# Refilling the gather indices of an edge loop by SyncE transfers inside SBUF instead of GpSimd copies

## The reference

```python
proj = (x @ Wp.T).reshape(-1, H, FO)                      # 6250 x 8 x 32
s = leaky_relu(scores_src[src] + scores_trg[trg], 0.2)    # one score an edge and head
exp_s = exp(s - max(s))
denom = segment_sum(exp_s, trg, N)
out = segment_sum(proj[src] * (exp_s / (denom[trg] + 1e-16))[:, :, None], trg, N)
```

## Time and profile before

| what | value |
|---|---|
| time, median of 3 runs | 3241.75 us (3241.1 to 3244.08) |
| profiled execution: span from the first to the last instruction | 3796.4 us |
| of it the edge loop, first gather to the end of the last | 247.76 to about 2809 us |
| busy in the whole span: PE, DVE, ACT, POOL | 56%, 52%, 23%, 48% |

### The profile page before, as it was taken

The page is one execution under the profiler, slowest core; times in us unless marked ns, Lnnn a source line. Parts: engine busy times, 40 slices in busy tenths (PEclk is TensorE's granted clock), DMA queues, the critical chain, the costliest instruction groups (busy, mean ns, idle before and its releaser), DMA issues. The chain is left out here.

```text
span 3796.4 us, 46157 instructions
## 1 busy us (share of the span) xinstructions
PE 2122.9 (56%) x12432; PEld 1788.7 (47%) x12433; DVE 1956.5 (52%) x5386; ACT 890.4 (23%) x2271; POOL 1821.9 (48%) x2025
## 2 busy tenths in 40 slices
PE   3755454544545554545455455444543359999990
PEld 3434343433434443434334334333433359999990
DVE  6545444444444444444444444444458746666654
ACT  1221111111111111111111111111114435555540
POOL 1026655656556656656565565655635722222110
PEclk7976767677777667677677776776765579999995
DMA  1333322323233333323333333322324442222116
GB/s 54 113 96 84 86 80 81 85 78 85 80 81 83 86 83 85 84 81 83 81 84 81 81 83 83 85 80 80 85 63 144 117 118 65 68 90 67 44 44 207
DMA packets 163652, 326.51 MB, mean 86 GB/s; under 512 B 41487, under 2 KB 95742, under 8 KB 163628
## 3 DMA queue, kind: packets, MB, share of 16 engines
q0 software_dynamic: 98560, 256.53, 24.7%
q1 hardware_dynamic: 45528, 50.33, 4.4%
q10 hardware_dynamic: 19540, 19.40, 1.6%
HBM read 278.03 MB, written 47.99 MB: 86 GB/s over the span
## 5 line engine op out<-in xcount | busy, mean ns | idle before, releaser
L626 POOL DMA_INDIRECT rows<-proj_table,idx x1568 | 1492.1, 952 | 1028.6 <-DVE weighed L741 612.9
L670 PE MATMUL banks<-weighed,onehot 128*128 128x264 f32 x3136 | 1147.8, 528 | 1293.5 <-DVE weighed L741 1232.4
L670 PEld LDWEIGHTS banks<-weighed,onehot 128*128 128x128 f32 x3136 | 783.1, 263 | 1475.0 <-issue 1312.5
L725 DVE TENSOR_REDUCE target<-banks 128x32 f32<-128x96 f32 x393 | 100.6, 256 | 1193.0 <-remote 1108.5
L741 DVE TENSOR_TENSOR weighed<-rows,banks 128x1024 f32<-128x1024 f32 x392 | 474.5, 1211 | 0.0
L845 ACT ACTIVATE banks<-score,neg_bound 128x32 f32<-128x32 f32 x392 | 114.1, 291 | 1387.8 <-DVE score L734 1069.5
L840 ACT CAST onehot_t<-banks 128x512 bf16<-128x512 f32 x395 | 228.2, 578 | 764.3 <-remote 740.0
L1441 POOL DMA_INDIRECT results_by_token<-yrow,goes_to x104 | 109.1, 1049 | 478.2 <-DVE yrow L1389 350.7
L707 DVE TENSOR_TENSOR onehot<-banks,key_tab 128x512 f32<-128x512 f32 x397 | 270.9, 683 | 0.0
L1328 ACT ACTIVATE hid<-banks,params 128x256 f32<-128x256 f32 x416 | 197.9, 477 | 267.5 <-PE banks L1284 261.1
L1284 PE MATMUL banks<-f_xth,w1h 128*128 128x256 f32 x832 | 236.4, 284 | 27.2 <-ACT hid L1328 14.9
(11 more groups left out here) (236 smaller groups left out, 2901.1 us busy)
## 6 DMA issues: line engine op xcount, KB each, us to landing
rows<-proj_table,idx POOLq DMA_INDIRECT x1568
w_raw<-in_L_ffn_W_dram POOLq DMA_DIRECT2D x16, 1024.0 KB
xrow<-tokens_by_expert SPq DMA_DIRECT2D x106, 128.5 KB
c_y<-results_by_token SPq DMA_DIRECT2D x10, 1120.0 KB
proj_table<-trow ACTq DMA_DIRECT2D x50, 128.9 KB
xin<-in_x_dram SPq DMA_DIRECT2D x50, 125.0 KB
skip_rows<-srow ACTq DMA_DIRECT2D x50, 125.0 KB
r_skin<-skip_rows SPq DMA_DIRECT2D x10, 625.0 KB
```

The costliest lines, as they stand in the source:

```text
L626: nc.gpsimd.indirect_dma_start(rows[k][:, i, :], None, table, bass.IndirectOffsetOnAxis(ap=idx[pair][:, col:col + 1], axis=0)).then_inc(ga ...
L670: mm = nc.tensor.matmul(acc_bank[u // 2 % 2][:, 0:ROW], onehot[u][:, i, :], weighed[:, k * SET + i, :], start=(u % 2 == 0 and i == 0), sto ...
```

## The change

The four copies of a round leave GpSimd. SyncE gets a loop of its own over the rounds. For each pair it waits until the gathers of both its sets have landed (the semaphores `gathered`, which DVE waits for too), and then refills that `idx` tile for the next round by a transfer from `src_tab`, inside SBUF: 128 partitions of 32 bytes. The first four tiles are filled by four such transfers ahead of the loop. GpSimd waits, at the first set of each pair as before, for `idx_ready[pair]`, which now counts 16 a transfer. The table's tail is made long enough for the refill behind the last round (32 columns instead of 24). Behind a pass GpSimd also waits for those last refills, and SyncE waits for `forgotten` before it goes on.

```diff
             act.wait_ge(src_out, EC)
-            nc.scalar.copy(m["src_tab"][:, STEPS * G:(STEPS + AHEAD) * G], m["src_tab"][:, 0:AHEAD * G])
+            nc.scalar.copy(m["src_tab"][:, STEPS * G:STEPS * G + ROUND * SET], m["src_tab"][:, 0:ROUND * SET])
...
             def body(c, it, w):
                 at = counts(pool, c, 2)
-                one_more = value_of(pool, c + 1)
-
-                def sources(pair):
-                    nc.gpsimd.tensor_copy(idx[pair][:], m["src_tab"][:, bass.ds(ROUND * SET * it + pair * 2 * SET, 2 * SET)]
-                                          ).then_inc(idx_ready[pair], 1)
-
-                sources(0)
+                copied = value_of(pool, 16 * c + 16)
                 for u in range(ROUND):
                     k, pair = u % BUF, u // 2
                     pool.wait_ge(begun, 1)
                     if u % 2 == 0:
-                        pool.wait_ge(idx_ready[pair], one_more)
+                        pool.wait_ge(idx_ready[pair], copied)
                     pool.wait_ge(weigh_done[k], at(u))
...
-                    if u % 2 == 0 and u + 2 < ROUND:
-                        sources(pair + 1)
 
             def forget_gathers(w):
                 used = value_of(pool, 2 * IT * (w + 1) + 1)
+                copied = value_of(pool, 16 * IT * (w + 1) + 16)
                 pool.wait_ge(begun, 1)
+                for pair in range(ROUND // 2):
+                    pool.wait_ge(idx_ready[pair], copied)
...
         @block.sync
         def _(sp):
+            def sources(pair, first):
+                sp.dma_start(idx[pair][:], m["src_tab"][:, bass.ds(first + pair * 2 * SET, 2 * SET)]
+                             ).then_inc(idx_ready[pair], 16)
+
+            def body(c, it, w):
+                landed = [value_of(sp, 16 * SET * (2 * it + q + 1)) for q in range(2)]
+                following = sp.snap(ROUND * SET * it + ROUND * SET)
+                for pair in range(ROUND // 2):
+                    for u in (2 * pair, 2 * pair + 1):
+                        sp.wait_ge(gathered[u % BUF], landed[u // BUF])
+                    sources(pair, following)
+
+            def forget_landings(w):
+                passed = value_of(sp, w + 1)
+                sp.wait_ge(forgotten, passed)
+                sp.sem_inc(resumed, 1)
+
+            for pair in range(ROUND // 2):
+                sources(pair, 0)
             for done in m["spent_by_nodes"]:
                 sp.sem_clear(done)
+            over_passes(sp, body, forget_landings)
```

More of the change, by code:

```diff
@@ L52 @@
 COLS = EC * P * Q
-assert (STEPS + AHEAD) * G <= COLS
+assert (STEPS + AHEAD) * G <= COLS and STEPS * G + ROUND * SET <= COLS
 NO_NODE = 16384
@@ L583, in edge_phase @@
             "st_picked", "st_ready", "acc_added", "max_masked", "max_kept"))
-        peak_dve, peak_pe, windows_moved, forgotten = (sem(s) for s in (
-            "peak_dve", "peak_pe", "windows_moved", "forgotten"))
+        peak_dve, peak_pe, windows_moved, forgotten, resumed = (sem(s) for s in (
+            "peak_dve", "peak_pe", "windows_moved", "forgotten", "resumed"))
         begun = m["begun"]
```

## The result

The changed kernel takes 3191.64 us (median of 4 runs, 3190.28 to 3194.89) against 3241.45 before: 0.9842 of the time, 95% interval 0.983 to 0.9853. It is 49.8 us faster. The forecast was 3206 us and 36 us; its lowest end, 3191 us of 3241.75, is a ratio of 0.9843, just above what was measured.

What follows compares the result with a forecast made beforehand. POOL was taken to pace the edge loop in the timed runs. Mid-round copies -13, copies at the turn -32, SyncE's issues +7 and the start +2 gave -36 us, so 3206 us (1.1% less); range 3191 to 3242.

Steps and rivals of the forecast that it cites:

- the copies at the turn: Edge loop, top of each round: 48 copies on POOL at 0.67 us each, 32 us gone; other end 10 us.
- POOL paces the timed loop: Edge loop: a POOL that never waits takes 2011 us; the profile's 550 us more are pauses absent from timed runs.
- Rival A: Edge loop: waits for DVE and PE also fill timed runs, a quarter of the saving or less left, 3232 to 3242; chance 0.12.
- Copies by their place: POOL's gathers in the edge loop: a copy costs 0.67 us at the turn of a round, 0.09 in mid-round.
- The mid-round copies: Edge loop, three copies a round on POOL, 147 in all at 0.09 us each: 13 us gone.
- SyncE's issues: Edge loop, 196 refills issued beside POOL's gathers: 0.035 us each, +7 us (0 to +69).
- The start: Ahead of the loop: the first gather now waits for a transfer, +1 to +3 us, taken as +2.
- The profiled span: Profile after the change: falls by far less than 36 us; wait for weighed rows grows over 612.9 us.
- Slack of the refill: SyncE's refills in the loop: due 30 us later, landing 2.4 to 3.9 us after issue, some 24 us free.

## Why the prediction was right, and where it was wrong

The mechanism held, and the size did not: 36 us were forecast and 49.8 measured, a ratio of 0.9842 just past the 0.9843 of the range's lowest end. The step that failed is the term for the copies at the turn. It was put at 32 us, with 10 as its other end, and measured 36 to 38.

**POOL paces the timed loop: right, shown.** The forecast rested on taking the profiled execution's 550 us of pauses for something that the timed runs don't have. The profile taken again has a loop of 2013 us, within 2 us of the sum over POOL's distances. Rival A falls. That the sums met so closely was in part luck. The plain distance is 1.250 us in that profile and not 1.254, 6 us less over the loop, and the turns cost 6 us more than the sum gave them. Outside the loop the two executions differ too: 1226 us, where the prediction took the 1235 of the first profile for both.

**Copies by their place: right, shown.** 0.67 us at the turn, 0.09 to 0.10 in mid-round, as read. The wait for a copy just made is dear, not the turn.

**What is off is sizes.** 49.8 - 36 = 14 us were missed, in three terms that together make 15. The mid-round copies are 14 us by the rows where 13 stood. A few us go the other way: the changed kernel's distances are 1.2527 us on the mean, and the plain ones of the second profile of before 1.250. That isn't SyncE's doing, as the two variants with as many of its issues or four times as many have 1.2508 and 1.2505, and the two profiles of before differ by as much (1.253 and 1.250).

- *SyncE's issues, +7 us: measured 0.* The 0.03 us came from three distances of another phase, with other work around them. In the changed kernel, distances with an issue of SyncE are no longer than those without, and 588 more issues changed nothing.
- *The start, +2 us: measured about 0.* From the ACT table load that opens the block, the first gather came 248.10 - 245.53 = 2.57 us later in the kernel before. After, the load is at 244.26 and the gather at 246.93: 2.67 us. SyncE issued the first refill at 244.24, while POOL had come to its own first copy only 1.42 us behind the load (246.95). The prediction had put the transfer's landing behind the place of the copy, not beside what POOL did before it, and even its least value of +1 was too high.
- *Copies at the turn, -32 us: measured -38 by the rows, -36 by the run with these copies back.* The term was 48 x 0.67 from one turn, and that part is confirmed. What it left out stands one gather later: 0.02 us at every turn, 1 us in all, and 5.2 us at the three turns where a gap of 2.04 us follows. All three gaps were in the trace of before as well. They were missed because only the turn's own distance was read, at one turn. The term had room towards 10 us only, so the lowest end of the sum, -44, could not reach what was measured.

The loop closes the account: 2013 us before, 1964 after, 49 us. Taking parts back gives 36 for the turns and 11 for mid-round.

**The profiled span** was to fall by far less than the time, since pauses would take up the gain. It fell by 607 us, as the pauses didn't come again, and the wait for weighed rows, which was to grow over 612.9 us, is 59.4. A profile with pauses was taken to be how this kernel is always profiled; one execution can't tell that.

**Slack of the refill: right.** A refill landed in 2.6 us (1.7 to 3.7) where 2.4 to 3.9 had been assumed, and 20 us less slack changed nothing. The rule from the Trainium skill, that transfers of SyncE and GpSimd interleave on the same engines (DMA: Bandwidth & Descriptors, Issuing engines are not separate DMA queues), had no price that any run shows here, even with four transfers for one.

## What to carry to other kernels

Where a profiled span is far above the timed runs, sum the pacing engine's distances and see whether they meet the timed runs, before believing the table of waits. On an engine that issues one transfer after another, look for the instruction that waits for one just issued on the same engine. Making what it waits for a few instructions earlier brought 36 of the 50 us here with no new engine. And a term that is "so many times one row" should be checked by summing all of the rows, with the rows just behind them, as three odd turns of 48 made a tenth of this gain.

## What was not expected of the hardware

At every 104th gather from 113 on a gap of 2.04 us can stand on POOL, 1.74 more than the usual 0.30, and no row names what fills it. It shows only where the gather before had to wait, whatever for. The first profile of before has it at seven of these fourteen gathers (113, 321, 529, 737, 945, 1153, 1361), each behind a gather that had waited, six of them for over 5 us. At the other seven the gather before had not waited, and there is none. The first of the seven:

```profile
426.94 0.94 POOL L626 DMA_INDIRECT rows<-proj_table,idx  x1 [5.92 <-DVE weighed L741]
429.96 0.96 POOL L626 DMA_INDIRECT rows<-proj_table,idx  x1 [2.08 <-issue]
```

In the changed kernel gather 737 follows the one before it as any other does:

```profile
1169.03 0.95 POOL L620 DMA_INDIRECT rows<-proj_table,idx  x1 [0.30 <-issue]
1170.28 0.95 POOL L620 DMA_INDIRECT rows<-proj_table,idx  x1 [0.30 <-issue]
```

Some work on POOL's side every 104 gathers, hidden by a lead of its sequencer over the gathers that a wait uses up, would explain both; no run here shows it. The Trainium skill, Perfetto Trace Analysis (DMA Instruction — SWDGE (GPSIMD)), has the sequencer push such an instruction into a wait queue and go on to the next, and the copies that start at the very end of a gather agree with it. What is done every 104 gathers stays open, as does what made the pauses of the first profile.
